# Four projections of a token-mixing stage: float32 products replaced by float16 high and low halves

## The reference

```
xxx   = xn + dx * maa_x
m     = tanh(xxx @ maa_w1)            # 5 x 32 columns
lerp_i = xn + dx * (maa_stack_i + m_i @ maa_w2_i)       # i = w, k, v, r, g
decay = exp(-exp(time_decay + tanh(lerp_w @ decay_w1) @ decay_w2))
k = lerp_k @ Wk ;  v = lerp_v @ Wv ;  r = lerp_r @ Wr ;  g = silu(lerp_g @ Wg)
```

## Time and profile before

| | |
|---|---|
| median of 3 runs | 5390.73 us (5383.15 to 5391.22) |
| the profiled execution's own time | 5388.99 us |
| its span, first to last instruction | 5387.2 us |
| mean granted TensorE clock | 0.957 of full |
| busy: TensorE, VectorE, ScalarE, GpSimd | 4900.7 (91%), 3663.5 (68%), 2863.8 (53%), 1945.1 us (36%) |
| first stages, 0 to 400 us: TensorE, VectorE, ScalarE, GpSimd | 341.07, 231.87, 143.14, 0.20 us |

### The profile page before, as it was taken

How to read it: one execution, slowest core, us unless ns; L and a number is a source line. 1 busy time by engine, 2 the same in 40 slices (tenths; PEclk the granted TensorE clock), 3 DMA queues, 4 the chain that set the end, 5 groups by cost and what they waited for, 6 DMA issues and landing times. The chain is left out here.

```text
span 5387.2 us, 74684 instructions
## 1 busy us (share of the span) xinstructions
PE 4900.7 (91%) x28562; PEld 1738.7 (32%) x28562; DVE 3663.5 (68%) x4647; ACT 2863.8 (53%) x5370; POOL 1945.1 (36%) x900
## 2 busy tenths in 40 slices
PE   6997999999598799997999999997899999996899
PEld 2432334434233233332322222222343333331344
DVE  5658898988444577772499999994367777771431
ACT  2433443444222266665288888886225666665432
POOL 0006566665000277886000000000007888886000
PEclk9997999999799799999999999998899999998999
DMA  2334333333211333321311111111424323221200
GB/s 98 121 113 124 106 97 103 101 105 94 92 55 39 77 69 79 75 56 53 121 33 35 33 32 32 34 33 56 122 71 98 71 60 79 58 50 69 70 24 16
DMA packets 466031, 384.00 MB, mean 71 GB/s; under 512 B 174511, under 2 KB 363796, under 8 KB 465512
## 3 DMA queue, kind: packets, MB, share of 16 engines
q1 hardware_dynamic: 465664, 379.13, 25.9%
HBM read 242.83 MB, written 135.14 MB: 70 GB/s over the span
## 5 line engine op out<-in xcount | busy, mean ns | idle before, releaser
L2721 DVE TENSOR_REDUCE att_part<-att_scores 128x2 f32<-128x802 f32 x1024 | 953.1, 986 | 106.0 <-PE att_scores L2560 94.0
L2694 ACT ACTIVATE att_prob<-att_lower 128x512 f32<-128x512 f32 (+1 forms) x1664 | 882.9, 596 | 124.8 <-PE att_lower L2574 103.8
L3490 DVE TENSOR_REDUCE att_part<-att_scores 128x1 f32<-128x423 f32 x1280 | 675.8, 590 | 241.6 <-PE att_scores L3221 241.4
L1292 POOL TENSOR_TENSOR scan_z<-scan_r,scan_states 128x512 f32<-128x512 f32 x256 | 450.5, 1764 | 776.5 <-DVE scan_states L1368 770.8
L3434 ACT ACTIVATE att_prob<-att_lower 128x512 f32<-128x512 f32 (+1 forms) x1088 | 563.4, 602 | 243.9 <-PE att_lower L3233 242.1
L3474 POOL TENSOR_TENSOR att_acc<-att_acc,att_prob 128x1024 f32<-128x1024 f32 (+2 forms) x240 | 671.5, 2798 | 51.7 <-ACT att_prob L3434 22.6
L2297 DVE TENSOR_REDUCE att_part<-att_scores 128x1 f32<-128x401 f32 x1024 | 515.4, 567 | 162.5 <-PE att_scores L2111 162.4
L2589 PE MATMUL att_lower<-att_prob,att_v 128*32 128x256 f32 (+1 forms) x6144 | 520.9, 411 | 19.7 <-issue 19.7
L2236 ACT ACTIVATE att_prob<-att_scores 128x512 f32<-128x512 f32 (+1 forms) x832 | 430.8, 601 | 195.8 <-PE att_scores L2123 195.7
L2277 POOL TENSOR_TENSOR att_acc<-att_acc,att_prob 128x1024 f32<-128x1024 f32 (+2 forms) x176 | 450.2, 2558 | 69.0 <-ACT att_prob L2236 56.0
L2708 POOL TENSOR_TENSOR att_out<-att_sums_sb,att_spread 128x512 f32<-128x512 f32 x32 | 40.7, 1273 | 1161.6 <-DMA att_spread<-recips 1161.6
(11 more groups left out here) (350 smaller groups left out, 7636.5 us busy)
## 6 DMA issues: line engine op xcount, KB each, us to landing
v<-scan_val SPq DMA_DIRECT2D x96, 256.0 KB, 2.3
att_v<-v SPq DMA_DIRECT2D x32, 768.0 KB
att_spread<-recips SPq DMA_DIRECT2D x64, 256.0 KB
mix_plane<-in_mask SPq DMA_DIRECT2D x16, 800.5 KB, 6.5
att_k<-k1hi SPq DMA_DIRECT2D x32, 400.2 KB
att_k<-k3hi SPq DMA_DIRECT2D x32, 400.2 KB
scan_x<-in_ctx_t SPq DMA_DIRECT2D x12, 1024.0 KB, 5.7
o<-att_out SPq DMA_DIRECT2D x32, 256.0 KB, 2.0
```

Source lines behind the costliest of these rows:

```text
L1292: nc.gpsimd.tensor_tensor(Z[n % ZR][:], src["r"][n // HS % 2][:], S[n % SR][:, 0:T], ALU.mult).then_inc(zdone, 1)
L2694: nc.scalar.activation(prob[g % NP][0:kw(kt), h, :], scores2[0:kw(kt), n % RING2, :], ACT.Exp).then_inc(exped, 1)
L2721: nc.vector.reduce_max(part[q % 2][:, :, ec, piece], scores1[:, bank["unit", p], :, 0:PIECE], AX.X).then_inc(reduced, 1)
L3490: nc.vector.reduce_max(part[q % 2][:, hc, piece:piece + 1], scores1[:, bank["piece", p], 0:PIECE], AX.X).then_inc(reduced, 1)
```

## The change

The four projections take float16 halves of weights and lerps instead of float32 tiles.

- Weights: the float32 weights are loaded into tiles that are free at the start (`raw`). ScalarE rounds each to its high half before the drains of the first `lora`; VectorE forms the low halves (three at the first `lora`, `Wg` at the first `decay1`).
- Lerps: ScalarE forms the high half of lerp 0 at the head of `mix23`, of lerp 2 behind the first and of lerp 3 behind the last drain of `key`, of lerp 4 behind the third drain of `recept`. VectorE forms the low half of lerp 0 at the end of `mix10`, of lerp 2 at `key`, of lerp 3 at `decay2`, of lerp 4 at `recept`, each at the head of its item.
- A group is now 12 float16 matmuls. The drains divide by `WSCALE`.
- Lerp 4 shares its tiles with lerp 0, and its halves with those of lerp 2. VectorE interpolates lerp 0 before lerp 1, and `decay1` waits for both.
- New waits: `key` for `keyhalf`, the other projections for `half234`, ScalarE's rounding for `mixed` and for the projection that read the tile last.

```diff
-        W = {n: ph.sb(n, [P, C, E]) for n in ("Wr", "Wk", "Wv", "Wg")}
+        W = {n: Halves(ph.sb(n + "h", [P, C, E], F16), ph.sb(n + "l", [P, C, E], F16)) for n in ("Wk", "Wv", "Wr", "Wg")}
...
-        lerp = [ph.sb(f"lerp{i}", [P, C, T]) for i in range(5)]
+        lerp = [ph.sb(f"lerp{i}", [P, C, T]) for i in range(4)]
+        lerp.append(lerp[0])
+        half = [Halves(ph.sb(f"half{i}h", [P, C, T], F16), ph.sb(f"half{i}l", [P, C, T], F16)) if i in (0, 2, 3) else None
+                for i in range(4)]
+        half.append(half[2])
+        raw = {"Wk": y[0][:], "Wv": y[1][:], "Wr": dx[1][:], "Wg": xn[1][:, :, 0:E]}
...
-        ORDER = (1, 0, 2, 3, 4)
+        ORDER = (0, 1, 2, 3, 4)
...
 # TensorE
-                        pe.wait_ge(mixed, 5 * b + 1)
+                        pe.wait_ge(mixed, 5 * b + 2)
                         group([(dw1[:, c, :], lerp[1][:, c, :]) for c in range(C)], m=64)
...
                         if b == 0:
-                            pe.wait_ge(wloaded[weight], 16)
-                        pe.wait_ge(mixed, 5 * b + ORDER.index(i) + 1)
+                            pe.wait_ge(wlow, list(W).index(weight) + 1)
+                        if i == 0:
+                            pe.wait_ge(keyhalf, b + 1)
+                        else:
+                            pe.wait_ge(half234, 3 * b + i - 1)
                         for o in part:
-                            group([(W[weight][:, c, o * P:(o + 1) * P], lerp[i][:, c, :]) for c in range(C)])
+                            group(split_pairs([(W[weight][:, c, o * P:(o + 1) * P], half[i][:, c, :]) for c in range(C)]))
...
 # ScalarE
+                def weight_high(n):
+                    act.wait_ge(wloaded[n], 16)
+                    nc.scalar.activation(W[n].hi[:], raw[n], ACT.Identity, scale=WSCALE).then_inc(whigh, 1)
+
+                def lerp_high(b, i):
+                    act.wait_ge(mixed, 5 * b + ORDER.index(i) + 1)
+                    if i == 4:
+                        act.wait_ge(product, ends[b, "value"])
+                    elif b:
+                        act.wait_ge(product, ends[b - 1, {0: "key", 2: "gate", 3: "recept"}[i]])
+                    nc.scalar.activation(half[i].hi[:], lerp[i][:], ACT.Identity).then_inc(round234 if i else keyround, 1)
...
+                        else:
+                            for n in W:
+                                weight_high(n)
...
-                        if b:
-                            act.wait_ge(product, max(ends[b - 1, n] for n in (("decay1", "key") if what == "mix10" else ("value", "recept"))))
+                        if b and what == "mix10":
+                            act.wait_ge(product, ends[b - 1, "decay1"])
+                            act.wait_ge(half234, 3 * b)
+                        elif b:
+                            act.wait_ge(half234, 3 * b - 1)
+                        if what == "mix23":
+                            lerp_high(b, 0)
...
-                        if b:
-                            act.wait_ge(product, ends[b - 1, "gate"])
+                        act.wait_ge(keyhalf, b + 1)
...
                             for o in part:
-                                drain(dst[:, o, :], ACT.Silu if what == "gate" else ACT.Identity)
+                                drain(dst[:, o, :], ACT.Silu if what == "gate" else ACT.Identity, scale=1.0 / WSCALE)
+                                for i in {("key", 0): (2,), ("key", C - 1): (3,), ("recept", 2): (4,)}.get((what, o), ()):
+                                    lerp_high(b, i)
...
 # VectorE
+                def weight_low(n):
+                    dve.wait_ge(whigh, list(W).index(n) + 1)
+                    nc.vector.scalar_tensor_tensor(W[n].lo[:], raw[n], WSCALE, W[n].hi[:], ALU.mult, ALU.subtract).then_inc(wlow, 1)
+
+                def lerp_low(b, i):
+                    dve.wait_ge(round234, 3 * b + i - 1)
+                    nc.vector.tensor_tensor(half[i].lo[:], lerp[i][:], half[i].hi[:], ALU.subtract).then_inc(half234, 1)
...
                 for b, what, part in order():
+                    if what == "key":
+                        lerp_low(b, 2)
+                    elif what == "decay2":
+                        lerp_low(b, 3)
+                    elif what == "recept":
+                        lerp_low(b, 4)
...
-                        for i in {"mix10": (1, 0), "mix23": (2, 3), "mix4": (4,)}[what]:
+                        for i in {"mix10": (0, 1), "mix23": (2, 3), "mix4": (4,)}[what]:
                             interpolate(b, i)
+                        if what == "mix10":
+                            dve.wait_ge(keyround, b + 1)
+                            if b:
+                                dve.wait_ge(product, ends[b - 1, "key"])
+                            nc.vector.tensor_tensor(half[0].lo[:], lerp[0][:], half[0].hi[:], ALU.subtract).then_inc(keyhalf, 1)
+                    elif b == 0 and what in ("lora", "decay1"):
+                        for n in {"lora": ("Wk", "Wv", "Wr"), "decay1": ("Wg",)}[what]:
+                            weight_low(n)
```

More of the change, by code:

```diff
@@ L191, in rwkv_inputs @@
             ph.sem(n) for n in ("centred", "squared", "totalled", "shifted", "mixed", "decayed", "reduced", "marked", "made", "flagged"))
-        ORDER = (1, 0, 2, 3, 4)
+        whigh, wlow, keyround, keyhalf, round234, half234 = (
+            ph.sem(n) for n in ("whigh", "wlow", "keyround", "keyhalf", "round234", "half234"))
+        ORDER = (0, 1, 2, 3, 4)
         OUTS = {"key": (0, "s_k", "Wk"), "decay2": (1, "s_w", None), "value": (2, "s_v", "Wv"), "recept": (3, "s_r", "Wr"),
@@ L258, in _ @@
                 load_weight("dw", dw2[:], w["decay_w2"])
-                load_weight("Wk", W["Wk"][:], chunked(w["Wk0"]))
+                load_weight("Wk", raw["Wk"], chunked(w["Wk0"]))
                 load_x(1)
                 for n in ("Wv", "Wr", "Wg"):
-                    load_weight(n, W[n][:], chunked(w[n + "0"]))
+                    load_weight(n, raw[n], chunked(w[n + "0"]))
                 load_plane(0)
@@ L382, in _ @@
                             act.wait_ge(stored[n % 2], 16 * (n // 2))
+                        elif n == 1:
+                            act.wait_ge(wlow, 2)
                         dst = y[n % 2]
@@ L418, in _ @@
                             dve.wait_ge(mixed, 5 * (b - 1))
+                        elif b:
+                            dve.wait_ge(wlow, 4)
                         link(nc.vector.tensor_copy(xnb[:, :, 0], prev[:, b, :]))
```

## The result

| | before | after |
|---|---|---|
| median | 5390.73 us (5 runs, 5383.15 to 5392.31) | 5416.78 us (5 runs, 5412.89 to 5418.03) |
| span of the profiled execution | 5387.2 | 5415.7 |
| last projection of the first stage ends | 394.63 | 421.87 |
| starts of `key` in the four batches | 80.44, 166.51, 249.22, 331.94 | 84.50, 175.30, 265.58, 356.23 |

The ratio of the runs is 1.0049, 95% interval 1.0038 to 1.0060: slower by 26 us, 0.5%, where the forecast was 5413 (terms that add up to +23). Of the 28.5 us between the two spans 27.2 arise in the first stage; what comes behind it takes 4993.8 us against 4992.6.

The account below looks back on a forecast made before the run. TensorE bounds the first stage before; afterwards waits through VectorE and ScalarE do. Terms 4.4 - 1.25 + 3.2 + 16.8 = +23.2 on 5389.0 give 5412.2, a little more for the median: 5413 us, range 5394 to 5432.

Parts of the forecast that it names:

- TensorE saves 53.8 us of work: First-stage projections: 64 groups, each 2.59 us instead of 3.43, the most that the change can bring.
- The ring: Each batch: waits through VectorE and ScalarE replace TensorE's bound, period 83.25 to 83.5 us; three periods change by -1.25.
- Start, +4.4: Before the first `key`: `decay1` waits for two interpolations, so `key` starts at 84.8 instead of 80.44 us.
- End, +3.2: Last batch: `gate` waits 14.3 us for low half 4 behind four planes; `key` to end 65.9 us, before 62.7.
- Clock, +16.8: After waits before `mean`, `gate` and `decay1`: clock falls to 1.2 GHz, costing 5.6 us a batch, three times.
- the forecast's signs: What the profile after would show, among it a batch period of 87 to 90 us, clock below 1 in three places.
- TensorE as the bound: First-stage batches: TensorE's 69.2 us against VectorE's 64.9 sets the batch, kernel at 5340; chance 4%.
- the clock that doesn't fall: Batch waits: the three times 5.6 us vanish, kernel at 5395; chance 10%.
- The clock stays low longer: Batches: nine more low stretches at 1.7 us, or planes that come late, kernel at 5428; chance 15%.
- Closer spacing: Float16 matmuls in the batches and the end: 131 ns apart instead of 0.216 us, 43 us less, 5370; chance 1%.

Follow-up runs that it names:

- the third experiment: The changed kernel with the third product of each triple (low weights by high lerps) left out in `recept` alone: 5414.3 us, ratio to before 1.0045.
- the filled kernel: The changed kernel with overwritten matmuls put into TensorE's waits before `mean`, `gate` and `decay1`: 5395.2 us, ratio to before 1.0012.
- the chunks first: The changed kernel with VectorE summing the next x's chunks at the head of `key`, before any low half: 5400.7 us, ratio to before 1.0023.
- with GpSimd: The changed kernel with the low half of lerp 4 formed by GpSimd instead of VectorE: 5392.3 us, ratio to before 1.0003.

## Why the prediction was right

- *TensorE saves 53.8 us of work.* Right, and worth nothing by itself: a float16 group takes 12 x 0.216, and the shorter `recept` of the third experiment made no period shorter.
- *The ring.* Right to 0.2 us: 83.4 with the clock held, against 83.25 to 83.5. Its legs are right too, within 0.3 us, so the match isn't luck: from `key` to `mean`, on to `gate`, on to the next `key` it is 17.2, 41.8 and 24.4 us in batch 2 of the filled kernel, for 17.35, 41.8 and 24.1 to 24.35. In the changed kernel the waits are within 0.2 us of their forecast; only the one before `lora` stands in one batch of three, since I had not thought of a low stretch in `recept`.
- *Start, +4.4.* It was +4.06 (84.50 for 84.8): `decay1` starts 0.26 later than worked out and takes 5.14 us instead of 5.73.
- *End, +3.2.* 65.6 from `key` to the end for 65.9 in the forecast, +2.9 on the 62.7 before. The last `gate` starts 53.2 after `key` (53.1).
- *Clock, +16.8.* The mechanism was right, the size too small. The three periods add up to 271.7, less the ring's 250.25: 21.5, or 7.2 a batch for 5.6. I had priced `mean` and `decay1` at one stretch of 3.4 us each, from the earlier trace rows; here the stretches were 6.8 long (but for `decay1`'s in batch 1), in batch 2 with 4.6 and 5.9 us of matmuls in them. Half of the matmul time in the three stretches of batch 2 is 2.3 + 2.4 + 2.9 = 7.6, near the 7.2. The batch period came out at 90.3 to 90.8, above the 87 to 90 of the forecast's signs, for this reason. The trace of before had a case of the longer kind, which I hadn't weighed; its wait and its window:

```profile
666.27 2.07 PE L1091 MATMUL scan_psum<-scan_total,const_mean 128*128 128x512 f32 x2 [2.47 <-POOL scan_total L1305]
```

```profile
666.30:673.00 6.70, 6.70 (x13) 2.20 (x14) 4.01 (x7) 0.69 (x2) 1.80 (x2) 0.50 0.53 164
```

- The sum of the first-stage terms was +23.2 against +27.2 measured there: 4.7 more for the clock, 0.6 less for start and end. In the medians it is 5413 for 5416.8.
- *The rivals.* TensorE as the bound (5340) and the clock that doesn't fall (5395) are refuted by the runs above; the second is just what the filled kernel shows, 5395.2. "The clock stays low longer" (5428) was partly true: the stretches at `mean` and `decay1` were the longer ones but for one, those at `gate` were as priced. That second rival had as support that pieces with 32 rows had passed at full clock; that holds for the earlier trace rows, but not for batch 0 of the kernel before, shown above. Closer spacing: 48 matmuls of `key` fill 10.5 us, 0.216 each as in the earlier trace rows, in a stream with weight loads. The figure of 131 ns in the Trainium skill ("TensorE: Matmul & The Clock Gate", section "Back-to-back issue gap") isn't borne out here; in the traces, before and after, no two float16 matmuls of 128 rows and 512 columns start less than 0.215 us apart.

Of the falls of the clock on the ring, shown is that they come at the waits and go when the waits are filled. Which waits bring one stays open (2.59 us did in most batches and didn't in two, 3.4 us did in two batches and didn't in one), and how long it lasts, 3.4 or 6.8 us. Why `recept` runs low behind `mix4` in some batches and not in others stays open as well.

## What to carry to other kernels

When an engine is full before a change, work out the ring of waits that would be left, at full clock, before counting on its saved work: here 54 us of matmuls went and the batch stayed at 83 even at full clock, chiefly because a new 2.3 us step had been put behind 7 us of work that nobody waits for. Where a new step lands in a strict queue matters more than its price; moved ahead of the mask planes and behind the next sum, the same instructions make the kernel faster by 0.5%. The waits of 2.6 us and more on TensorE cost their length and in most cases here 1.4 to 3 us more by the lower clock.

## What the runs showed of the hardware

- At waits of only 2.58 to 3.04 us the clock was at half for 6.8 us in five of six cases of the changed kernel, for 3.4 us in one. Two waits of 2.59 us (one with the chunks first, one with GpSimd) and one of 3.36 us (with GpSimd) passed at full clock.
- The clock also falls with no wait before it: in the kernel before, for 6.8 us from 116.7 on, with TensorE busy all through, behind matmuls of 32 rows.
- Matmuls whose results are thrown away keep the granted clock at 1.00 through waits that otherwise take it to 0.50, 7.2 us a batch.
- A GpSimd subtraction of 128x2048 float32 and float16 into float16 takes 4.06 us, 1.8 times VectorE's 2.29.
